# Shared-expert products, the last batches' routing and the row norms rescheduled in a fused attention and mixture-of-experts kernel

## The chip, the core and the metric

The kernel runs on one core of one Trainium2 chip. The metric is the time of one execution on the device in microseconds (us). All engines of the core are named as in the profile: PE (TensorE, matrix products) with PEld (its weight loads), DVE (VectorE), ACT (ScalarE), POOL (GpSimd) and SP (SyncE, which here only issues transfers). Each engine works through its own instructions in order and waits on semaphores that other engines raise.

## The reference

Four stages change a residual `x` of 4 batches x 256 tokens x 256 features, each after a layer norm. The change touches the end of the third and the whole fourth stage:

```python
x = x + _L0_xattn_ref(_layernorm(x), ctx_2048, mask)          # one wide attention over 1601 rows
x = x + _L0_ffn_ref(_layernorm(x), ...)                        # 16 experts, dense, plus shared
x = x + _L1_xattn_ref(_layernorm(x), ctx_2048, mask, ...)      # 16 heads of 16, 1601 keys
x = x + _L1_ffn_ref(_layernorm(x), ...)                        # 16 experts, top 2, plus shared
...
# inside _L1_xattn_ref, at its end
delta = rs * (ctx @ Wo.T + bo)
delta = (delta - mu) / jnp.sqrt(var + EPS_LN) * ln_gamma + ln_beta
...
# inside _L1_ffn_ref
logits = flat @ router_w.T
scores = jax.nn.softmax(logits, axis=-1)
_, topk_idx = jax.lax.top_k(logits + router_bias, TOPK)        # TOPK = 2
...                                                            # weights: chosen scores, normalized
for e in range(N_EXPERTS):                                     # 16 experts of width 128
    h = jax.nn.silu(flat @ Wu[e]) * (flat @ Wg[e])
    out = out + combine[:, e:e + 1] * (h @ Wd[e])
out = out + jax.nn.silu(flat @ Su[0]) * (flat @ Sg[0]) @ Sd[0] # shared expert of width 256
```

## The kernel before

**The attention loop.** The third stage is one loop over 208 units: 16 jobs (4 batches x 4 groups of heads) of 13 tiles of keys. For each unit x PE makes scores (`qk(x)`, L881), ACT takes their exponential (L1279), DVE clips it (`clip(x)`, L1659), and PE multiplies with the values (`pv`, L915) four units later. After a job DVE copies the product out (`evac`, L1665), PE transposes it (`flip`, L923), and DVE divides (`norm`, L1672 to L1677), which raises `cx_rdy`. What follows for a batch b (its tokens are row tiles t = 2b and t + 1) is hidden in the units of batch b + 1 by functions called `between`, one on each engine, with an order written out by hand in unit numbers `o` of 52 per batch: context transposed (`ctx_T`, L930) and multiplied by Wo (`ctx_out`, L937), `delta` with its statistics, `delta_gamma` (L1695), `delta_add` into the residual (L1701), `rows_stat` (L1705), `rows_mean` (L1710) at o = 39, `rows` (L1718, the normalized rows `xe`) at o = 43 and 45, `rows_T` on PE (L944) at o = 49, `rows_hi` on ACT (L1259) at o = 49 and `rows_lo` on DVE (L1723) at o = 50, which split the transposed rows in a rounded part `xTh` and a rest `xTl`. Between `rows_mean` and `rows`, POOL finds the inverse root with 13 small instructions (`inverse_root`, L351 to L359). In the next batch's units follow the router logits, the choice of two experts (fifteen small DVE instructions, `logits_ev` to `take_both`), `ranks` (L960, L963: each token's place within its expert), `slots_of` and `slots_to` (row addresses), and `rows_out` on POOL: four indirect transfers (L621) that scatter the two row tiles, 128 rows each, to each token's two places in the memory tensor `x_slots`.

**After the loop.** Batch 3 has no later units to hide in, and batch 2's choice is also made there. In order of the DVE: norm of the last job, `delta` and statistics, `delta_gamma`, `delta_add`, the row norms (here ACT takes the root), `rows`, `rows_lo`, then the choice for the four row tiles of batches 2 and 3 in one go, their slots, the counts (`all_counts`, L1046) turned into a list of 31 blocks of 128 slots (`nblk_` to `rb_i`, L1890 to L1913), in between and after it the shared expert's hidden products in four chunks (`shared_chunk`, L1899 and L1901), the softmax weights (`m_sum` to `m_w2`), and four additions of the shared expert's result to the residual (L1934). PE meanwhile makes the transposes and logits, 16 products with zeros that start the eight accumulators (L1015), and `shared_hidden(n)` (gate and up products, 6 matrix products each, of 512 tokens) and `shared_down(n)` (12 products). Each float32 product of this stage is made of three (`mm3`, L646, L647, L648) from rounded parts and rests. The shared expert's weights come with the expert weights when the loop has ended (SP waits for `cx_rdy`), and POOL splits them (`sh_hi` L633, `sh_lo` L635).

**The expert blocks.** For each of 31 blocks: SP loads 128 rows from `x_slots` (L544; it waits first for all scatters and for the block list), PE transposes them (L1064), gate and up product (L1078), ACT silu, DVE product (L1938), PE transpose and down product (L1092), DVE copy (L1949), POOL scatters them to `y_tokens` (L641). Then SP loads all rows back (`yg`), and DVE adds them to the residual with the softmax weights (L1963, L1965).

## Time and profile before

| | |
|---|---|
| median of 3 runs | 817.32 us (817.09 to 819.99) |
| the profiled execution, its own time | 816.02 us |
| its span, first to last instruction | 814.2 us |
| busy: PE, DVE, ACT, POOL | 707.8, 543.3, 396.5, 160.1 us |
| mean granted TensorE clock | 0.950 of full speed |
| attention loop, first exponential to the last job's context | 463.8 to 690.7 us |
| from there to the first expert block's gate and up product | 690.7 to 742.3 us |
| 31 expert blocks, to the last scatter issued | 742.3 to 798.0 us |

Times within the profile count from the span's first instruction. The shares are averages over four different stages, so that the table only says that PE works most of the time; what a microsecond is worth is read stage by stage.

### The profile page before, as it was taken

The numbers are of one execution on the slowest core, as the hardware profiler recorded it, in microseconds if no ns is written. First come the engines' busy times: TensorE is split into PE (matmuls) and PEld (weight loads), VectorE is DVE, ScalarE is ACT, GpSimd is POOL, SyncE is SP. The second block draws the span as 40 slices with busy tenths as digits, with TensorE's granted clock in tenths as the row PEclk, the third lists the DMA queues.
The fourth block names the chain that finished last, engine by engine and source line by source line (L and its number), as shares of the span: only waits on it lengthen the run. The fifth ranks groups of instructions, "written<-read, shape, count | busy, mean of one in ns | idle before, by whom it ended". The sixth has DMA issues, their size and how long they took to land.

```text
span 814.2 us, 14794 instructions
## 1 busy us (share of the span) xinstructions
PE 707.8 (87%) x5481; PEld 537.1 (66%) x5481; DVE 543.3 (67%) x1124; ACT 396.5 (49%) x558; POOL 160.1 (20%) x196
## 2 busy tenths in 40 slices
PE   4799999897859999999995599998998997587990
PEld 3689888796648888888885344454554554475880
DVE  6765565656676666666676377778888886655663
ACT  2624333233312322223322499999999996114540
POOL 5452625030100000000000000004024024231561
PEclk9999999998989999999998789999999998698995
DMA  7465464735306776767779369898687700812545
GB/s 231 129 208 214 162 220 130 270 104 178 96 23 221 238 248 206 262 211 245 240 172 198 60 112 191 133 127 166 96 137 144 108 2 30 345 53 74 162 144 180
DMA packets 57532, 131.67 MB, mean 162 GB/s; under 512 B 12433, under 2 KB 32785, under 8 KB 53889
## 3 DMA queue, kind: packets, MB, share of 16 engines
q1 hardware_dynamic: 54208, 123.46, 57.1%
q0 software_dynamic: 2256, 6.18, 2.1%
q10 hardware_dynamic: 1008, 1.25, 0.5%
q8 instruction: 37, 0.61, 0.4%
q14 instruction: 23, 0.18, 0.1%
HBM read 78.92 MB, written 48.79 MB: 157 GB/s over the span
## 4 chain that ended last, share of the span: by engine, by line
PE 53%; DVE 15%; issue 10%; ACT 9%; POOL 7%; DMA 4%; SPq 1%; POOLq 0%; DVEq 0%; ACTq 0%
PE ps L646 13%; PE ps L647 13%; PE ps L648 13%; ACT p L1279 5%; PE ps L915 5%; PE ps L881 3%; POOL y_tokens L641 3%; DVE p L1659 2%; DMA raw<-in_ctxT 1%; PE ps L1078 1%; DMA raw<-in_ctxN 1%; ACT cNh L1156 1%; PE ps L937 1%; PE ps L723 1%; POOL na L354 1%
## 5 line engine op out<-in xcount | busy, mean ns | idle before, releaser
L1279 ACT ACTIVATE p<-ps,kbias 128x1024 f32<-128x1024 f32 (+1 forms) x208 | 210.5, 1184 | 6.2 <-PE ps L881 6.2
L1659 DVE TENSOR_SCALAR p<-p 128x1024 f32<-128x1024 f32 (+1 forms) x208 | 142.6, 692 | 40.0 <-ACT p L1279 38.4
L915 PE MATMUL ps<-p,vsl 128*17 128x256 f32 (+1 forms) x1664 | 116.7, 392 | 3.6 <-DVE p L1659 3.6
L881 PEld LDWEIGHTS ps<-qst,kst 48*128 48x128 f32 (+1 forms) x832 | 60.4, 187 | 67.3 <-issue 34.6
L881 PE MATMUL ps<-qst,kst 48*128 48x256 f32 (+1 forms) x832 | 93.4, 324 | 11.5 <-DMA qst<-ql 5.9
L1219 ACT ACTIVATE hh<-h 128x512 fp32r<-128x512 f32 x50 | 31.6, 632 | 137.7 <-DVE h L1591 113.9
L351 POOL TENSOR_SCALAR nv<-mv 128x2 f32<-128x2 f32 x6 | 3.4, 561 | 423.7 <-DVE mv L1691 407.7
L646 PE MATMUL ps<-xTh,w_hi 128*128 128x512 f32 x200 | 80.0, 400 | 5.2 <-DVE h L1587 4.5
L648 PE MATMUL ps<-xTh,w_lo 128*128 128x512 f32 x200 | 79.3, 397 | 0.0
L647 PE MATMUL ps<-xTl,w_hi 128*128 128x512 f32 x200 | 79.2, 396 | 0.0
L915 PEld LDWEIGHTS ps<-p,vsl 128*17 128x17 f32 (+1 forms) x1664 | 37.2, 98 | 43.0 <-issue 9.1
L1593 DVE TENSOR_TENSOR hl<-h,hh 128x512 fp32r<-128x512 f32 x50 | 34.6, 692 | 36.6 <-ACT hh L1219 36.6
L646 PE MATMUL ps<-w_hi,hh 128*128 128x256 f32 x200 | 57.5, 288 | 1.5 <-DVE hl L1593 1.5
L1587 DVE TENSOR_TENSOR h<-silu,ps 128x512 f32<-128x512 f32 x50 | 34.4, 688 | 35.4 <-PE ps L648 23.2
L647 PE MATMUL ps<-w_lo,hh 128*128 128x256 f32 x200 | 57.2, 286 | 0.0
L648 PE MATMUL ps<-w_hi,hl 128*128 128x256 f32 x200 | 57.0, 285 | 0.0
L646 PEld LDWEIGHTS ps<-xTh,w_hi 128*128 128x128 f32 x200 | 37.9, 190 | 13.5 <-DVE h L1587 5.8
L589 POOL TENSOR_TENSOR cNl<-raw,cNh 128x1024 fp32r<-128x1024 f32 (+1 forms) x16 | 31.3, 1980 | 77.8 <-ACT cNh L1156 77.8
L648 PEld LDWEIGHTS ps<-xTh,w_lo 128*128 128x128 f32 x200 | 37.8, 189 | 9.0
L647 PEld LDWEIGHTS ps<-xTl,w_hi 128*128 128x128 f32 x200 | 37.9, 189 | 6.6
L646 PEld LDWEIGHTS ps<-w_hi,hh 128*128 128x128 f32 x200 | 38.7, 193 | 4.2 <-DVE hl L1593 1.9
L1215 ACT ACTIVATE silu<-ps 128x512 f32<-128x512 f32 x50 | 29.9, 598 | 21.6 <-PE ps L648 20.9
(290 smaller groups left out, 1530.0 us busy)
## 6 DMA issues: line engine op xcount, KB each, us to landing
x_slots<-blank SPq DMA_DIRECT2D x20, 1032.0 KB, 6.0
kst<-k_hi SPq DMA_DIRECT2D x64, 200.2 KB, 7.8
w_raw<-in_w SPq DMA_DIRECT2D x25, 384.0 KB, 3.6
v_one<-vst SPq DMA_DIRECT2D x4, 1768.0 KB, 9.0
vsl<-v_one SPq DMA_DIRECT2D x4, 1768.0 KB, 16.5
kst<-k_lo SPq DMA_DIRECT2D x32, 200.2 KB, 8.2
raw<-in_ctxN SPq DMA_DIRECT2D x12, 512.0 KB, 5.6
k_hi<-kh SPq DMA_DIRECT2D x24, 256.0 KB, 2.6
```

Of the source, the lines that this page charges most:

```text
L589: pool.tensor_tensor(cNl[:, c0:c0 + w, :], src, cNh[:, c0:c0 + w, :].bitcast(F32), ALU.subtract).then_inc(ctx_split, 1)
L646: e.matmul(o, lh, rh, start=first, stop=False, skip_group_check=True)
L647: e.matmul(o, lh, rl, start=False, stop=False, skip_group_check=True)
L648: return e.matmul(o, ll, rh, start=False, stop=last, skip_group_check=True)
L881: mm = pe.matmul(ps[0:rows, 2 * (x % RING) + t, c * SEQ:(c + 1) * SEQ], kst[r, job % KSL, c, m * P:m * P + rows], qst[r, b, 2 * g + c, :], ...
L915: mm = pe.matmul(ps[32 * j:32 * j + VW, 6 + job % 2, 0:SEQ], vsl[0:rows, b % 2, at_:at_ + VW], p32[0:rows, x % PBUF, (2 * t + c) * SEQ:(2 ...
L1215: act.activation(silu[:, half, :], ps[:, 4, :], ACT.Silu).then_inc(silu_rdy, 1)
L1219: act.activation(hh[:, half, :], h32[:, half, :], ACT.Copy).then_inc(hh_rdy, 1)
L1279: act.activation(p32[0:rows, x % PBUF, :], psf[0:rows, bank * 512:bank * 512 + 1024], ACT.Exp, scale=0.25, bias=kbias[0:rows, col:col + 1] ...
L1587: dve.tensor_tensor(h32[:, half, :], silu[:, half, :], ps[:, 5, :], ALU.mult).then_inc(mul1_rdy, 1)
L1593: dve.tensor_tensor(hl[:, half, :], h32[:, half, :], hh[:, half, :].bitcast(F32), ALU.subtract).then_inc(hl_rdy, 1)
L1659: dve.tensor_scalar(t, t, CLO, CHI, ALU.max, ALU.min).then_inc(p_clip, 1)
```

## The change

1. **Row norms.** `rows_mean` at o = 38 (was 39), `rows` at 45 and 46 (were 43 and 45), `rows_T` at 51 (was 49), `rows_hi` at 50 (was 49), `rows_lo` at 51 (was 50).
2. **Shared weights early.** SP loads them at the loop's first unit into `xn`, which is free then. DVE splits them with eight instructions in units 2 to 9 of job 2. SP's load after the loop and POOL's four instructions are gone.
3. **Batch 2 on its own.** Its logits go first in PE's order after the loop, DVE makes its choice ahead of `delta`, and its ranks, slots and scatter have steps of their own. The choice, slots and scatter of batch 3 follow later for two row tiles.
4. **Shared products by 512 tokens.** The first 512 tokens (batches 0 and 1) are ready in full before the loop ends. PE makes three of their four products (`gates(0,0)`, `ups(0,0)`, `gates(0,1)`) ahead of the last `rows_T`. The down products of a half are made in one go of 24 (`shared_down`), they start their own accumulators, and the 16 products with zeros are gone.
5. **Softmax weights last.** The exponential and DVE's eleven instructions on the softmax come after the expert blocks. The additions to the residual are spread: an expert block waits only for the addition that frees its accumulator.
6. Buffers move in SBUF, and the hidden tiles have four chunks (were two).

```diff
@@ sync
             for g in range(NG - 1):
                 queries(0, g)
+            sp.wait_ge(sc_rdy, 1)
+            for k in range(NSH1):
+                sp.dma_start(sh_raw[:, k * WC:(k + 1) * WC], a["w1"][k]).then_inc(d_in[0], 16)
...
             sp.wait_ge(cx_rdy, NJ)
-            for k in range(NSH1):
-                sp.dma_start(e_w[:, k, :], a["w1"][k]).then_inc(d_in[0], 16)
@@ gpsimd
-            for k in range(NSH1):
-                pool.wait_ge(d_in[0], 16 * NSH1)
-                pool.tensor_copy(sh_hi[:, k, :], e_w[:, k, :]).then_inc(d_w, 1)
-                pool.wait_ge(d_w, 2 * k + 1)
-                pool.tensor_tensor(sh_lo[:, k, :], e_w[:, k, :], sh_hi[:, k, :].bitcast(F32), ALU.subtract).then_inc(d_w, 1)
+            rows_out(NB - 1, NT - 4, NT - 2)
             pool.wait_ge(ln_xn, 4 * NT)
-            rows_out(NB - 1, NT - 4, NT)
+            rows_out(NB, NT - 2, NT)
@@ tensor, after the loop
             t = NT - 2
+            logits(NB - 2, ps[:, 5, :])
             pe.wait_ge(cx_rdy, NJ)
             for j in range(2):
                 ctx_T(t + j, 1, ps[:, j, :])
-            logits(NB - 2, ps[:, 7, :])
             for j in range(2):
                 ctx_out(t + j, j, 1, ps[:, 2 + j, 0:D])
+            ranks(NB - 1, NT - 4, NT - 2, ps[:, 1, :])
+            pe.wait_ge(d_w, 8)
+            gates(0, 0, 4)
+            ups(0, 0, 5)
+            gates(0, 1, 6)
+            pe.wait_ge(dl_ev, NT)
             for j in range(2):
-                rows_T(t + j, 1, ps[:, 4 + j, :])
-            logits(NB - 1, ps[:, 7, 2 * E:])
-            for n in range(4 * 4):
-                pe.matmul(psf[:, n * P:(n + 1) * P], zero[:], zero[:], start=True, stop=False, skip_group_check=True)
...
+                rows_T(t + j, 1, ps[:, 2 + j, :])
+            ups(0, 1, 0)
+            logits(NB - 1, ps[:, 7, :])
+            pe.wait_ge(silu_rdy, SC0 + 1)
+            gates(1, 0, 4)
+            pe.wait_ge(mul1_rdy, SC0 + 1)
+            ups(1, 0, 5)
+            pe.wait_ge(silu_rdy, SC0 + 2)
+            gates(1, 1, 6)
+            pe.wait_ge(pre_ev, NB - 1)
+            ranks(NB, NT - 2, NT, ps[:, 1, :])
+            pe.wait_ge(lg_ev, NB)
+            all_counts(ps[:, 7, 2 * E:3 * E])
+            pe.wait_ge(mul1_rdy, SC0 + 2)
+            ups(1, 1, 0)
+            pe.wait_ge(hl_rdy, SC0 + 2)
+            shared_down(0, 2)
+            pe.wait_ge(hl_rdy, SC0 + 4)
+            shared_down(1, 6)
@@ vector, in the loop and after it
-                    elif o == 39:
+                    elif o == 38:
                         rows_mean(b)
-                    elif o == 43:
+                    elif o == 45:
                         rows(t)
-                    elif o == 45:
+                    elif o == 46:
                         rows(t + 1)
-                    elif o == 50:
+                    elif o == 51:
                         rows_lo(t, 2, spare)
...
+                if job == 2 and 2 <= m < 10:
+                    (shared_hi if m < 6 else shared_lo)(m)
...
+            choose(t - 2, t, ps[:, 5, :])
             for j in range(2):
                 delta(t + j, 1, ps[:, 2 + j, :])
...
             rows(t + 1)
+            dve.wait_ge(pre_rdy, NB - 1)
+            slots_of(t - 2, t, ps[:, 1, :])
             for j in range(2):
-                rows_lo(t + j, 1, ps[:, 4 + j, :])
+                rows_lo(t + j, 1, ps[:, 2 + j, :])
+            slots_to(t - 2, t)
...
+            shared_mul(0, 5)
+            choose(t, NT, ps[:, 7, :])
+            shared_mul(1, 0)
             dve.wait_ge(pre_rdy, NB)
+            slots_of(t, NT, ps[:, 1, :])
+            slots_to(t, NT)
+            shared_low(0)
+            shared_low(1)
+            dve.wait_ge(pre_rdy, NB + 1)
...
+            for q in range(4):
+                x = resid[:, 2 * q:2 * q + 2, :].rearrange("p t d -> p (t d)")
+                dve.wait_ge(down_done, SC0 + q // 2 + 1)
+                dve.tensor_tensor(x, x, ps[:, (2, 3, 6, 7)[q], :], ALU.add).then_inc(add_rdy, 1)
```

## Rows read from the trace of the kernel before

**Rows 1.** Windows: from:to, length, busy us (count) per engine, clock, DMA share, GB/s.
```profile
695.00:700.00 5.00, 0.00 (x0) 0.00 (x0) 4.89 (x9) 0.30 (x1) 4.72 (x4) 0.80 1.00 396
...
705.00:710.00 5.00, 4.74 (x23) 4.77 (x23) 1.75 (x9) 0.00 (x0) 0.00 (x0) 0.50 1.00 391
...
750.00:797.00 47.00, 44.77 (x244) 36.97 (x242) 27.54 (x109) 22.10 (x81) 28.09 (x30) 1.00 0.50 147
```

**Rows 2.** Chain that ended last, pieces after the loop: start, us, what.
```profile
712.43 0.43 PE ps L648
...
733.86 1.28 ACT L1304
...
738.51 2.49 DVE resid L1934 x4
...
753.05 0.87 PE ps L1078 x4
...
754.67 0.86 PE ps L1078 x4
...
801.04 4.95 DMA yg<-y_tokens
```

**Rows 3.** Timeline, end of the loop: start, us, instruction, [idle before <-releaser].
```profile
656.82 24.14 ACT L1279 ACTIVATE p<-ps,kbias 128x1024 f32<-128x1024 f32 x24 [0.61 <-PE ps L881]
...
678.68 0.41 DVE L1718 TENSOR_SCALAR xe<-resid,mv,rstd 128x256 f32<-128x256 f32 x1 [2.02 <-POOL rstd L359]
...
682.75 0.60 ACT L1259 ACTIVATE xTh<-ps 128x512 fp32r<-128x512 f32 x1 [1.79 <-PE ps L944]
...
684.41 2.11 ACT L1279 ACTIVATE p<-ps,kbias 128x1024 f32<-128x1024 f32 x2 [1.06 <-PE ps L881]
...
689.05 0.42 DVE L1665 COPY oS<-ps 128x256 f32<-128x256 f32 x1 [1.60 <-PE ps L915]
```

**Rows 4.** Timeline, row norms of batch 0 (569 us) and batch 1.
```profile
569.40 0.60 ACT L1259 ACTIVATE xTh<-ps 128x512 fp32r<-128x512 f32 x1 [0.53 <-PE ps L944]
...
625.72 0.60 ACT L1259 ACTIVATE xTh<-ps 128x512 fp32r<-128x512 f32 x1 [1.16 <-PE ps L944]
```

**Rows 5.** Timeline, DVE and POOL at the last norms.
```profile
693.75 0.48 DVE L1681 SCALAR_TENSOR_TENSOR xn<-ps,rs,bo 128x256 f32<-128x256 f32 x1 [3.02 <-PE ps L937]
...
695.82 2.42 DVE L1695 SCALAR_TENSOR_TENSOR xn<-xn,mv,gam 128x256 f32<-128x256 f32 x2
...
696.02 1.94 POOL L635 TENSOR_TENSOR sh_lo<-e_w,sh_hi 128x768 fp32r<-128x768 f32 x1
...
698.35 2.79 DVE L1701 SCALAR_TENSOR_TENSOR resid<-xn,rstd,resid 128x256 f32<-128x256 f32 x2
...
702.65 0.74 DVE L1718 TENSOR_SCALAR xe<-resid,mv,rstd 128x256 f32<-128x256 f32 x2
...
704.26 0.85 DVE L1723 TENSOR_TENSOR xTl<-ps,xTh 128x256 fp32r<-128x256 f32 x2 [0.88 <-ACT xTh L1259]
```

**Rows 6.** Timeline, from the choice to the first expert block.
```profile
708.00 0.22 DVE L1744 COPY m_l<-ps 128x64 f32<-128x64 f32 x1 [2.89 <-PE ps L648]
...
711.54 0.23 DVE L1768 TENSOR_TENSOR sel<-one 128x64 fp32r<-128x64 f32 x1
...
718.24 0.17 DVE L1780 CAST pos_i<-pos_f 128x8 int32<-128x8 f32 x1
...
728.22 1.01 POOL L621 DMA_INDIRECT x_slots<-xe,pos_i  x1 [0.30 <-issue]
...
731.76 14.84 SPq L544 DMA_DIRECT2D xb<-x_slots  x7
...
742.32 2.07 PE L1078 MATMUL ps<-e_w,xbT 128*128 x4 [0.15 <-ACT xbT L1308]
```

**Rows 7.** Group of DVE instructions by form, over the span: count, busy us, mean ns.
```profile
L1901 DVE TENSOR_TENSOR hl_d<-h_d,hh_d 128x512 fp32r<-128x512 f32 x4 | 2.8, 692 | 2.8 <-ACT hh_d L1302 1.4 <-issue 1.4
```

**Rows 8.** The same view, from 600 to 690 us, in the loop.
```profile
L1695 DVE SCALAR_TENSOR_TENSOR xn<-xn,mv,gam 128x256 f32<-128x256 f32 x4 | 1.9, 479 | 0.0
```

More of the change, by code:

```diff
@@ L198, in build @@
             big_d = Dt("big_d", [P, NBLK, E])
[L199 to L201 removed]
+            m_p, m_e = Dt("m_p", [P, NT, E]), Dt("m_e", [P, NT, E])
+            eb_f = Dt("eb_f", [P, NBLK])
+            eb_i = Dt("eb_i", [P, NBLK], I32)
+            eb_r = Dt("eb_r", [P, NBLK])
+            y_c = Dt("y_c", [P, NBLK])
+            y_i = Dt("y_i", [P, NBLK], I32)
+            ob, rb_f = Dt("ob", [P, NBLK]), Dt("rb_f", [P, NBLK])
+            rb_i = Dt("rb_i", [P, NBLK], I32)
+            Dt("gap3", [P, 4050])
             gw_raw_d = Dt("gw_raw_d", [P, KT, E])
@@ L1002, in _, with gates, ups, shared_down @@
             flip(NJ - 1)
+            def gates(h, k, bank):
+                s = slice(h * 512, h * 512 + 512)
+                for q in range(KT):
+                    w = slice(q * 2 * P, q * 2 * P + P)
+                    mm = mm3(pe, ps[:, bank, :], sh_hi[:, k, w], sh_gl[:, k, w], xTh[:, q, s], xTl[:, q, s], q == 0, q == 1)
+                mm.then_inc(G_rdy, 1)
+            def ups(h, k, bank):
+                s = slice(h * 512, h * 512 + 512)
+                for q in range(KT):
+                    w = slice(q * 2 * P + P, (q + 1) * 2 * P)
+                    mm = mm3(pe, ps[:, bank, :], sh_hi[:, k, w], sh_gl[:, k, w], xTh[:, q, s], xTl[:, q, s], q == 0, q == 1)
+                mm.then_inc(U_rdy, 1)
+            def shared_down(h, bank):
+                for j in range(4):
+                    o = ps[:, bank + j // 2, (j % 2) * D:(j % 2 + 1) * D]
+                    s = slice(j * P, (j + 1) * P)
+                    for k in range(NSH1):
+                        mm = mm3(pe, o, hh_d[:, 2 * h + k, s], hl_d[:, 2 * h + k, s],
+                                 sh_hi[:, k, 2 * D:3 * D], sh_dl[:, k, :], k == 0, k == NSH1 - 1)
+                mm.then_inc(down_done, 1)
+            def all_counts(o):
+                for t in range(NT):
+                    mm = pe.matmul(o, ones[:], sel[:, t, :], start=t == 0, stop=t == NT - 1, skip_group_check=True)
+                mm.then_inc(pre_rdy, 1)
             t = NT - 2
+            logits(NB - 2, ps[:, 5, :])
             pe.wait_ge(cx_rdy, NJ)
@@ L1033, in shared_down @@
-            def shared_down(n):
-                k, half = n // 2, n % 2
-                pe.wait_ge(hl_rdy, SC0 + n + 1)
-                for j in range(4):
-                    t, s = 4 * half + j, slice(j * P, (j + 1) * P)
-                    mm = mm3(pe, ps[:, t // 2, (t % 2) * D:(t % 2 + 1) * D], hh_d[:, half, s], hl_d[:, half, s],
-                             sh_hi[:, k, 2 * D:3 * D], sh_lo[:, k, 2 * D:3 * D], False, False)
-                mm.then_inc(down_done, 1)
-            def all_counts():
-                cnt = ps[:, 7, 4 * E:5 * E]
-                for t in range(NT):
-                    mm = pe.matmul(cnt, ones[:], sel[:, t, :], start=t == 0, stop=t == NT - 1, skip_group_check=True)
-                mm.then_inc(pre_rdy, 1)
@@ L1049, in _ @@
-            shared_hidden(0)
-            ranks(NB - 1, NT - 4, NT, ps[:, 6, :])
-            all_counts()
-            for n in range(1, 2 * NSH1):
-                shared_hidden(n)
-                shared_down(n - 1)
-            shared_down(2 * NSH1 - 1)
+            ranks(NB - 1, NT - 4, NT - 2, ps[:, 1, :])
[4 more added lines that the diff above has]
+            pe.wait_ge(dl_ev, NT)
+            for j in range(2):
+                rows_T(t + j, 1, ps[:, 2 + j, :])
@@ L1293, in _, with shared_silu, shared_high @@
             for j in range(2):
-                rows_hi(t + j, 1, ps[:, 4 + j, :])
-            for n in range(2 * NSH1):
-                ct, half = SC0 + n, n % 2
-                act.wait_ge(G_rdy, ct + 1)
-                act.activation(silu_d[:, half, :], ps[:, 4, :], ACT.Silu).then_inc(silu_rdy, 1)
-                act.wait_ge(mul1_rdy, ct + 1)
-                if n >= 2:
-                    act.wait_ge(down_done, ct - 1)
-                act.activation(hh_d[:, half, :], h32_d[:, half, :], ACT.Copy).then_inc(hh_rdy, 1)
-            act.wait_ge(pos_rdy, NB)
-            act.activation(m_p[:].rearrange("p t e -> p (t e)"), m_e[:].rearrange("p t e -> p (t e)"), ACT.Exp).then_inc(s_exp, 1)
+                rows_hi(t + j, 1, ps[:, 2 + j, :])
+            def shared_silu(n, bank):
+                act.wait_ge(G_rdy, SC0 + n + 1)
+                act.activation(silu_d[:, n, :], ps[:, bank, :], ACT.Silu).then_inc(silu_rdy, 1)
+            def shared_high(n):
+                act.wait_ge(mul1_rdy, SC0 + n + 1)
+                act.activation(hh_d[:, n, :], h32_d[:, n, :], ACT.Copy).then_inc(hh_rdy, 1)
+            shared_silu(0, 4)
+            shared_silu(1, 6)
+            shared_high(0)
+            shared_silu(2, 4)
+            shared_high(1)
+            shared_silu(3, 6)
+            shared_high(2)
+            shared_high(3)
             def slots_ev(j):
```

139 lines of the change are left out of this document (67 added, 72 removed).

## The prediction

> **What bounds the kernel now.** First I read the timeline at the end of the attention loop. There ACT sets the pace: 24 exponentials follow each other without a gap, 1.006 us apart [rows 3]. Then ACT stands for 1.79 us until PE has transposed batch 2's normalized rows, and for 1.06 us more until PE has the next scores [rows 3]. PE is late because DVE is late: DVE stood 2.02 us for POOL's root ahead of `rows` [rows 3]. The same wait stands at the other two batches, with 0.53 and 1.16 us [rows 4]. So the loop is bound by ACT and has holes cut by the row norms.
>
> Second, the timeline and the windows after the loop. `cx_rdy` comes at about 690.7 (the last job's copy starts at 689.05 and flip and division take 1.7 us). The last norms run until DVE's `rows` end at 703.39 [rows 5]; for 695 to 700 us PE does nothing at all [rows 1], and this is the hole. PE then works at 1.2 GHz (clock 0.50 [rows 1]): a product of 128x512 takes 0.43 us [rows 2], half of it at 2.4 GHz. From 703.39 to the first expert product at 742.32 [rows 6] lies a chain of choice, slots, eight scatters, block list, shared products, softmax weights and additions. PE, the scatters and DVE all take part in it, and DVE's order decides: its four additions end at 741.0 [rows 2], and the expert blocks wait for the last.
>
> Third, the chain of waits in the expert blocks: one gate and up product starts 1.62 us after the other and nearly all pieces between are PE's [rows 2]. The change does not touch a block's work, so what is won before it is kept to the end, unless the clock changes.
>
> **Part by part.** Times on the right of an arrow are of the changed kernel, on the trace's time scale without what batches 0 and 1 give.
>
> *Row norms.* `rows_mean` comes a unit (1.0 us) earlier, so POOL's root is there a unit earlier, and DVE asks for it two units later. DVE's 2.02 us of waiting shrink to nothing. The second `rows` moves by one unit, PE's transposes by two, so that their rows lie ready about 2 us ahead. PE makes the last two scores ahead of the transposes, so that ACT needs no wait for either. Batches 0 and 1 give 0.53 + 1.16 = 1.7 us. What is queued behind the later `rows_T` are products with the values, which have four units of lead. For batch 2: exponential 205 ends at 680.96 [rows 3], then one exponential, `rows_hi` 0.60, the last exponential 1.0, clip 0.7, `rows_lo` 0.7: the last job's copy starts at 685.1 instead of 689.05, if PE stays at 2.4 GHz because its holes are gone. That gives 4.0 us; `cx_rdy` -> 686.8.
>
> *Shared weights in job 2.* Eight DVE instructions of 512 or 256 columns. The dearest kind near it, 128x512 from two inputs, takes 0.692 us [rows 7], so at most 5.5 us; I take 3.5, for half of them are casts and half are of 256 columns. DVE has 0.3 us free per unit (0.69 of 1.006), 2.4 us in eight units, less a norm, a copy and an addition. It falls behind by some 1.5 us, and the four units of lead cover this. Cost 0, at worst 3.5; I take 0.4. SP's two transfers of 0.4 MB each stand ahead of `keys(3)`, which waits for unit 13 anyway.
>
> *POOL's split is gone from the norms.* Two `delta_gamma` took 2.42 us and two `delta_add` 2.79 while POOL subtracted [rows 5]. In the loop one takes 0.479 [rows 8]. With pitches of 0.45 the four take 1.8 instead of 5.2: 3.4 us. The Trainium skill ("SBUF — State Buffer", Who interferes with whom) says that a DVE instruction with two SBUF inputs and a GpSimd instruction that reads SBUF exclude each other; the long rows agree. The same section says that descriptors of GpSimd's own DMAs can starve under DVE's copies; by that the scatters moved beside DVE's work would be longer, and I come back to it as a rival.
>
> *Batch 2's choice ahead of `delta`.* Its logits run after `flip`, in the 0.7 us until `cx_rdy` and a little beyond: 12 small products, 1.3 us -> done 687.4. Fifteen DVE instructions for four row tiles took 3.77 us (708.00 to 711.77 [rows 6]); for two tiles, with a pitch of 0.22, 3.3 -> 690.8. `delta` could have started at 689.2 (it waited for PE until 693.75 [rows 5]), so the choice delays it by 1.6. From there to the end of `rows` it was 9.64 us [rows 5], less 3.4 = 6.25 -> 697.05. From `cx_rdy` to `rows` it was 12.7 and becomes 10.3: 2.4 us.
>
> *Shared products in the hole.* After `ctx_out` (690.1) PE does six small rank products and 18 products of 128x512 at 0.23 us: 691.0 -> 696, before `rows_T` at 697. They fit, cost nothing on the path, and keep PE busy, so the later work should run at 2.4 GHz.
>
> *From `rows` to the first expert product.* `rows_lo` ends 1.7 us after `rows` as before [rows 5] -> 698.8. PE: `ups(0,1)` 1.3, logits 1.3 (2.9 before, at half the clock [rows 6]) -> 700.2 with the first product beginning while `rows_lo` still waits for `rows_hi`. Choice of two tiles 3.3 -> 703.5. PE has made three more chunks by 704.4, ranks 1.0 -> 705.4. Slots 0.8 and 0.6 -> `pos_i` 706.8 (718.41 before [rows 6]). Now DVE has 9.5 us without a pause: 17 instructions, of them four shared and three list ones of 0.67 to 0.71 us, by pitch: two rests 1.3, list to `off` 1.55, `end_` 0.25, product 0.7, `big_d` 0.7, product 0.7, `eb_f` 0.7, rest 0.7, the six small and two long ones to `rb_i` 2.25, last rest 0.7 -> 716.3. `shared_down(1)` waits for this last rest. Its 24 products of 128x256 are 2.8 us at 2.4 GHz and 5.1 at 1.2; PE has stood for about 5 us before it, as ahead of 742.32, where the clock was down: I take 4.4 -> 720.7. Transposes and copy 0.95 -> first expert product 721.65. From `rows` on that is 24.6 us instead of 38.9: 14.3 us. The softmax weights are part of it, 4.65 us between the table load and the additions [rows 2].
>
> *The scatters beside it.* Four instead of eight stand at the end. The pitch was 1.27; from `pos_i` 706.8 the last is issued by 712.5, and from the last issue's end (729.23) to SP's first load (731.76) it was 2.5 [rows 6] -> 715.1. Then SP needs `rb_i` (715.6) and a load, 3 us -> 718.7, under the 720.7 of PE, with 2 us to spare.
>
> *The blocks' start.* The first block's product took 2.07 us, later ones 0.87 [rows 2, 6]. With PE coming straight from `shared_down` the first blocks run at 2.4 GHz: 0.9 us.
>
> *Softmax weights last.* One exponential with its table load and eleven instructions, 4.65 us [rows 2], start on the old scale when ACT has done the last block, 31 blocks of 1.62 after 742.3 and an overlap of 1 to 2, near 794.6, so they end at 799.3. The loads of `yg` land at 806.0 [rows 2], the first near 803, so they cover it by 4 us. Without the cover it would cost those 4.65.
>
> *Sum.* 1.7 + 4.0 + 2.4 + 14.3 + 0.9 - 0.4 = 22.9 us, from 816.02 us of the profiled execution, 793.1. The median of before is 1.3 us above its profiled run, so 817.32 - 22.9 = 794.4; I say **794.5**. The terms with bounds: the loop's 5.7 may be 2 to 7; the split -3.5 to 0; `shared_down` +0.7 or -1.6; the hole's 3.4 from 2 to 4.
>
> **The rivals.**
>
> *The clock stays down through the hole.* For it: the clock did fall in this stretch, with a mean of 0.80 from 695 to 700 us and 0.50 from 705 on [rows 1]. Against it: it fell when PE had done nothing for some us, and this time is filled now. At 1.2 GHz the 18 products last 7.7 us instead of 4.2, `rows_T`, `ups` and logits 3 us more: the choice of batch 3 starts 5.3 us later: 799.8.
>
> *The loop gives nothing.* The wait moves with the norms: PE transposes in the last pair of units of a batch, ACT has two exponentials instead of three of lead, and waits again. For it: less lead. Against it: DVE's wait was the cause. 5.7 us stay in: 800.2.
>
> *The scatters become the bound.* POOL takes 1.01 us to issue one [rows 6]. Were each to be held up beside DVE so that it took 1.94, as POOL's subtraction did [rows 5], the first four (from 700.7) would end at 709.4 instead of 705.8, and the last four at 718.3. With 2.5 and 3 us for landing and load, PE would have its rows at 723.8 instead of 720.7: 797.6. For it: batch 2's four now lie beside DVE's densest work. Against it: the eight of before lay beside subtractions and products too, at 1.01.
>
> *Slower.* One mechanism: the expert blocks run at 1.2 GHz. They are PE's alone, 1.62 us each at clock 1.00 [rows 1, 2], so a block at half the clock would cost 1.6 us more. From 14 slow blocks of 31 on, the 22.9 us are eaten; all 31 give 844. For it: the new blocks follow on a wait of PE. Against it: before, the blocks began slow after such a wait too, and all from 750 us on ran at clock 1.00 [rows 1].
>
> *Nothing changes*: only if a wait of about 20 us took the place of the chain, and the profile shows none.
>
> **How the numbers follow.** Forecast 0.62, clock in the hole 0.15, loop gives nothing 0.12, scatters 0.07, slower 0.03, nothing 0.01. The likeliest has 790 to 798 from its bounds; the range takes in the two rivals near 800 and a few us for DVE's order: **790 to 803**. About 0.5% is what can be told from no change. Faster 0.96, same 0.01, slower 0.03.
>
> **What would show it.** Right: ACT without a wait before its last two exponentials; `delta_gamma` and `delta_add` at 0.48 us; clock 1.00 from `flip` to about 12 us after `rows`; the first expert product some 31 us after the last `cx_rdy` (51.6 before); DVE waiting for nothing of PE between `pos_i` and the last rest. Wrong: PE at 0.50 in the hole, ACT waiting for `rows_T` again, SP's first load later than `rb_i`, or DVE standing for logits longer than 3 us.

## The result and the profile after

| | before | after |
|---|---|---|
| median on the same chip, 4 runs each | 817.21 us (815.5 to 819.99) | 792.52 us (791.19 to 799.51) |
| ratio, 95% interval | | 0.971 (0.965 to 0.978) |
| the profiled execution, its own time and its span | 816.02, 814.2 us | 793.57, 791.8 us |

The prediction was 794.5 us, 790 to 803. To see where the time went, I cut each span at five events that any of these kernels has. The loop begins here with PE's first product on the queries' weights, ahead of the first exponential, and ends at the start of the last `cx`.

| stretch of the trace, us | before | after | change | predicted |
|---|---|---|---|---|
| span's start to the loop | 449.81 | 451.39 | +1.58 | 0 |
| loop | 240.63 | 234.77 | -5.86 | -5.7 + 0.4 |
| last `cx` to the first expert product | 51.88 | 35.14 | -16.74 | -16.7 (2.4 + 14.3) |
| first expert product to the first scatter into `y_tokens` | 6.86 | 5.31 | -1.55 | -0.9 |
| first to last of the 31 scatters | 47.87 | 48.22 | +0.35 | 0 |
| last scatter's issue to the end | 17.15 | 16.97 | -0.18 | 0 |

**End of the loop.** The timeline of ACT and of DVE in the kernel after, from 656 to 687 us; a row is start, duration, engine, line, and in brackets the idle time ahead of it with what ended it. They answer to [rows 3].

```profile
656.68 25.14 ACT L1294 ACTIVATE p<-ps,kbias 128x1024 f32<-128x1024 f32 x25 [0.62 <-PE ps L883]
681.62 0.68 ACT L1274 ACTIVATE xTh<-ps 128x512 fp32r<-128x512 f32 x1
682.11 1.19 ACT L1294 ACTIVATE p<-ps,kbias 65x1024 f32<-65x1024 f32 x1
...
679.24 0.41 DVE L1742 TENSOR_SCALAR xe<-resid,mv,rstd 128x256 f32<-128x256 f32 x1 [0.92 <-POOL rstd L364]
...
686.16 0.29 DVE L1701 TENSOR_TENSOR cx<-ps,r 128x128 f32<-128x128 f32 x1
```

ACT's waits of 1.79 and 1.06 us are gone: 25 exponentials, the copy `rows_hi` and the last exponential follow each other. DVE still stands for POOL's root, 0.92 us instead of 2.02. Its second `rows` end at 680.58 (680.17 + 0.41), PE transposes from 680.87 to 681.53, and ACT's copy starts at 681.62. Nobody is late, but the margins are 0.3 and 0.1 us and not the 2 us that the prediction gave the rows.

**The last norms.** The timeline of DVE, 692 to 697 us, which answers to [rows 5].

```profile
692.23 0.88 DVE L1719 SCALAR_TENSOR_TENSOR xn<-xn,mv,gam 128x256 f32<-128x256 f32 x2
...
693.22 0.88 DVE L1725 SCALAR_TENSOR_TENSOR resid<-xn,rstd,resid 128x256 f32<-128x256 f32 x2
...
695.62 0.74 DVE L1742 TENSOR_SCALAR xe<-resid,mv,rstd 128x256 f32<-128x256 f32 x2
```

The pairs that took 2.42 and 2.79 us beside POOL's subtraction take 0.88 each. This is 3.45 us, and `rows` end at 696.36.

**PE and its clock.** The windows of the kernel after, which answer to [rows 1] (busy time of each engine, then PE's granted clock, the share of the DMA engines' time, GB/s).

```profile
695.00:700.00 5.00, 4.27 (x26) 3.24 (x25) 3.42 (x14) 3.93 (x8) 0.69 (x1) 1.00 1.03 402
...
710.00:712.00 2.00, 0.51 (x5) 0.31 (x3) 1.93 (x4) 1.01 (x2) 1.69 (x2) 1.00 0.34 122
712.00:714.00 2.00, 0.00 (x0) 0.00 (x0) 1.90 (x6) 0.00 (x0) 0.43 (x1) 0.81 0.22 76
714.00:720.00 6.00, 4.76 (x22) 4.77 (x23) 2.79 (x8) 0.00 (x0) 0.00 (x0) 0.50 0.24 66
...
724.00:770.00 46.00, 46.00 (x253) 38.55 (x252) 28.37 (x113) 23.18 (x85) 25.96 (x27) 1.00 0.55 154
```

The hole is filled: clock 1.00 (2.4 GHz) where before it was 0.80 and then 0.50. It falls to 1.2 GHz once, in PE's wait for the last rest, and is up again when the blocks begin.

**From the addresses to the first block.** The chain of waits of the kernel after, 714 to 721 us.

```profile
714.41 0.18 DVE rb_i L1969
714.59 0.61 DVE hl_d L1939
...
715.24 0.58 PE ps L648
...
720.38 0.12 PE ps L650
720.75 0.39 ACT xbT L1330
721.15 0.15 issue
```

DVE's list and rests set the pace up to 715.2, then 24 down products that follow each other 0.213 us apart (the last three closer), and the first expert product starts at 721.30. SP's first load stood at 715.69, 1.1 us after the list was there:

```profile
711.46 0.97 POOL L627 DMA_INDIRECT x_slots<-xe,pos_i  x1 [0.31 <-issue]
...
715.69 3.74 SPq L550 DMA_DIRECT2D xb<-x_slots  x4
```

The last scatter's issue had ended 3.3 us before it. Where a scatter does set this load, it is 2.5 us, as before [rows 6], or 2.7, as in experiment 10, whose chain has 2.60 us from the issue of the last scatter until it has landed. By this the last one was there at about 714.06 (an estimate: 711.46 + 2.60), 0.5 us ahead of the end of `rb_i` (714.59). So the scatters are off the path, but by half a microsecond at this load.

### The profile page after: what moved, and what is told of

Same layout as the page of the kernel before. It is cut to its first block, busy times and chain, and to the rows that moved or that the text cites. A ratio compares the mean times of both kernels' runs of the same rounds, so it can differ in the third digit from the quotient of the medians.

```text
span 791.8 us, 14802 instructions
## 1 busy us (share of the span) xinstructions
PE 703.4 (89%) x5471; PEld 532.9 (67%) x5471; DVE 544.1 (69%) x1153; ACT 394.2 (50%) x557; POOL 164.9 (21%) x192
## 3 DMA queue, kind: packets, MB, share of 16 engines
HBM read 78.92 MB, written 48.79 MB: 161 GB/s over the span
## 4 chain that ended last, share of the span: by engine, by line
PE 56%; ACT 12%; DVE 11%; issue 10%; DMA 6%; POOL 4%; SPq 2%; POOLq 0%; ACTq 0%; DVEq 0%
PE ps L648 13%; PE ps L649 12%; PE ps L650 12%; ACT p L1294 8%; PE ps L917 5%; PE ps L1092 3%; PE ps L883 3%; DMA raw<-in_ctxN 2%; PE ps L1108 2%; DMA raw<-in_ctxT 2%; POOL cTl L608 1%; POOL cNl L595 1%; ACT cNh L1171 1%; PE ps L659 1%; DMA k_lo<-kl 1%
## 5 line engine op out<-in xcount | busy, mean ns | idle before, releaser
L1421 DVE SCALAR_TENSOR_TENSOR kl<-ps,bk,kh 128x512 fp32r<-128x512 f32 (+1 forms) x32 | 19.5, 631 | 30.8 <-ACT kh L1162 30.8
```

## The experiments

The executions of one set lie several us apart (791.19 to 799.51 us for the changed kernel), and two sets of one kernel differ too: the changed kernel gave 792.52 and, later, 794.51 us. The sets come from different chips: experiments 1 to 4 from one, 5, 6, the first 7 and 8 from another, and the second 7, 9 and 10 with the second set of the changed kernel from a third. So beside the medians I compare stretches of the traces, cut as above, and medians of different chips only by their ratio to the kernel before. "Loop" is the second stretch of the table, "middle" the third, "start" the fourth, "blocks" the fifth; medians are of 4 to 6 executions (10 in experiment 2), and each ratio is to the kernel before beside it.

| kernel | median, us | ratio to before (95%) | loop | middle | start | blocks |
|---|---|---|---|---|---|---|
| before | 817.21 | 1 | 240.63 | 51.88 | 6.86 | 47.87 |
| after | 792.52 | 0.965 to 0.978 | 234.77 | 35.14 | 5.31 | 48.22 |
| after, once more | 794.51 | 0.967 to 0.974 | 233.51 | 35.63 | 5.31 | 48.13 |
| 1 norms where they were | 802.56 | 0.975 to 0.985 | 242.41 | 34.96 | 5.29 | 52.12 |
| 2 norms alone, on before | 813.15 | 0.991 to 0.996 | 235.13 | 53.77 | 6.98 | 47.88 |
| 3 POOL beside the norms | 799.48 | 0.973 to 0.981 | 234.46 | 39.42 | 5.32 | 49.19 |
| 4 softmax weights first | 795.15 | 0.968 to 0.977 | 233.47 | 35.77 | 5.36 | 51.57 |
| 5 hole empty | 801.81 | 0.979 to 0.985 | 234.74 | 42.43 | 5.30 | 48.79 |
| 6 zeros in the hole | 798.79 | 0.976 to 0.982 | 234.49 | 38.90 | 5.30 | 50.63 |
| 7 zeros ahead of the down products | 797.04 | 0.975 to 0.979 | 233.48 | 33.56 | 5.28 | 50.61 |
| 7 once more | 794.82 | 0.965 to 0.973 | 237.51 | 33.16 | 5.26 | 48.97 |
| 8 last rest early | 794.11 | 0.969 to 0.974 | 234.80 | 33.74 | 6.81 | 50.36 |
| 9 last rest early, and zeros | 793.58 | 0.965 to 0.972 | 234.46 | 33.86 | 6.80 | 47.95 |
| 10 all eight scatters at the end | 797.51 | 0.971 to 0.978 | 233.49 | 37.53 | 6.80 | 47.94 |

**1. The norms where they were** (edit on the changed kernel, in the three `between` functions; experiment 2 is the reverse edit on the kernel before).

```diff
@@ tensor
-                    elif o == 51:
+                    elif o == 49:
                         pe.wait_ge(cx_rdy, y // MT)
                         rows_T(t, 2, spare)
@@ scalar
-                    elif o == 50:
+                    elif o == 49:
                         rows_hi(t, 2, spare)
@@ vector
-                    elif o == 38:
+                    elif o == 39:
                         rows_mean(b)
-                    elif o == 45:
+                    elif o == 43:
                         rows(t)
-                    elif o == 46:
+                    elif o == 45:
                         rows(t + 1)
-                    elif o == 51:
+                    elif o == 50:
                         rows_lo(t, 2, spare)
```

> The changed kernel with its row norms put back to the unit numbers of before (rows_mean 39, rows 43 and 45, transposes 49). Theory (DVE's wait for the root stops the loop): ACT waits again near 569, 625 and 682 us by 0.5, 1.2 and 1.8 us, PE falls to 1.2 GHz at the loop's end, and the kernel is 5.7 us slower than the changed one, so about 798.5 us and 18.8 us faster than before. Rival (the loop's gain came with another part, such as SP's order or the early weights): the time stays at 792.5 us.

> The kernel before with the new unit numbers of the row norms and nothing else. Theory: the same three waits go, the last job's context comes 5.7 us earlier, and the kernel takes 811.5 us (ratio 0.993). Rival (the later transposes only pay together with the rest): 817 us, ratio 1.000.

ACT's timeline at the loop's end, first experiment 1, then experiment 2:

```profile
684.74 0.60 ACT L1274 ACTIVATE xTh<-ps 128x512 fp32r<-128x512 f32 x1 [1.74 <-PE ps L946]
686.40 2.11 ACT L1294 ACTIVATE p<-ps,kbias 128x1024 f32<-128x1024 f32 x2 [1.06 <-PE ps L917]
```

```profile
656.96 25.16 ACT L1279 ACTIVATE p<-ps,kbias 128x1024 f32<-128x1024 f32 x25 [0.61 <-PE ps L881]
682.18 0.60 ACT L1259 ACTIVATE xTh<-ps 128x512 fp32r<-128x512 f32 x1
682.67 1.10 ACT L1279 ACTIVATE p<-ps,kbias 65x1024 f32<-65x1024 f32 x1
```

The waits come back with the old units and go with the new ones, on either kernel. The loop as a whole loses 7.6 us in experiment 1 and gains 5.5 in experiment 2, whose ratio of 0.993 is 5.4 us. But the loop's first units differ between traces whatever the norms: 13.9 or 15.2 us pass from its start to the first exponential, and the sixth to the eleventh exponential are 6.0 to 6.4 or 7.6 us apart (7.6 in the traces of the kernel after and of experiments 2 and 5, where PE's clock came up later). The stretch in which the norms lie, from the 93rd of the 208 exponentials to the last `cx`, is free of this. It takes 131.75 us before and 132.54 in experiment 1, 124.72 in both traces of the changed kernel, 124.69 to 124.96 in the other nine traces with its code, and 125.00 in experiment 2. So the new places are worth 7.0 us on this stretch, 6.8 of them on their own, and undoing them costs 7.8.

By the ratios (0.980 beside 0.971) experiment 1 as a whole is some 7 us slower than the changed kernel, more than the 5.7 expected. Its blocks also took 3.9 us longer (below), which the edit does not touch.

**3. POOL beside the norms.** POOL copies and subtracts the shared weights once more from the moment `delta` starts, into a tile of its own that nobody reads.

```diff
+            pool.wait_ge(d_w, 8)
+            pool.wait_ge(dl_ev, NT)
+            for k in range(NSH1):
+                pool.tensor_copy(spl[:], sh_hi[:, k, :].bitcast(F32)).then_inc(d_w, 1)
+                pool.wait_ge(d_w, 8 + 2 * k + 1)
+                pool.tensor_tensor(spl[:], sh_hi[:, k, :].bitcast(F32), sh_hi[:, 1 - k, :].bitcast(F32), ALU.subtract).then_inc(d_w, 1)
+                pool.wait_ge(d_w, 8 + 2 * k + 2)
             rows_out(NB - 1, NT - 4, NT - 2)
```

> The changed kernel, with two POOL casts and two POOL subtractions of 128x768 added at the last norms, started when DVE has made both deltas. Their result goes to an unused buffer. Theory (POOL and DVE's two-input instructions hold each other up): the two delta_gamma take some 2.4 us instead of 0.88 and the two delta_add 2.8 instead of 0.88, the path is 3.4 us longer, about 796 us. Rival (the long rows of before came from the weight transfers running at 400 GB/s, which run here too): the four stay at 0.48 us each and the time at 792.5 us.

DVE's timeline in it:

```profile
691.32 2.49 DVE L1728 SCALAR_TENSOR_TENSOR xn<-xn,mv,gam 128x256 f32<-128x256 f32 x2
...
693.92 2.84 DVE L1734 SCALAR_TENSOR_TENSOR resid<-xn,rstd,resid 128x256 f32<-128x256 f32 x2
```

The two pairs are back at 2.49 and 2.84 us, 3.6 more than 0.88 twice, and the middle is 4.3 us longer (3.8 beside the second trace of the changed kernel). Most of the rest is a wait of DVE of 0.64 us for PE's `ctx_out` ahead of the second `delta`, since PE's clock was 0.50 there. The weight transfers run beside the pairs in both kernels (402 GB/s from 695 to 700 us in the kernel after, where the pairs are fast), so they are not what made them long. The neighbour is the cause. The rule that the prediction took from the Trainium skill ("SBUF — State Buffer", Who interferes with whom) holds here in both directions: the same instructions, slow with POOL beside them, fast without.

**4. The softmax weights first.** The exponential and DVE's eleven instructions go back ahead of the four additions.

```diff
 @@ scalar, ahead of the expert blocks (was behind them)
+            act.wait_ge(pos_rdy, NB + 1)
+            act.activation(m_p[:]..., m_e[:]..., ACT.Exp).then_inc(s_exp, 1)
 @@ vector, ahead of the additions to resid (was behind the blocks)
+            dve.wait_ge(s_exp, 1)
+            link(dve.tensor_reduce(m_sum[:], m_p[:], AX.X, ALU.add))
...
+            link(dve.tensor_tensor(m_w2[:], m_w2[:], m_top[:], ALU.mult))
```

> The changed kernel with the softmax exponential and DVE's eleven softmax instructions put back ahead of DVE's four additions. Theory: they need 4.65 us, but shared_down(1) with its 5.3 us runs beside them, so that the additions of banks 6 and 7 end only 1 to 2 us later; with the silu table loaded again in the first block this makes 2 us, about 794.5 us. Rival (all 4.65 us were on the path, as the sum of the prediction took them): 797.2 us.

DVE's timeline in it, from the first to the last of the eleven and on to the additions:

```profile
712.44 0.29 DVE L1974 TENSOR_REDUCE m_sum<-m_p 128x8 f32<-128x128 f32 x1 [0.38 <-ACT m_p L1328]
...
715.26 0.17 DVE L1984 TENSOR_TENSOR m_w<-m_w,m_top 128x8 f32<-128x8 f32 x1
715.46 1.28 DVE L1988 TENSOR_TENSOR resid<-resid,ps 128x512 f32<-128x512 f32 x2
717.13 1.29 DVE L1988 TENSOR_TENSOR resid<-resid,ps 128x512 f32<-128x512 f32 x2 [0.38 <-PE ps L650]
```

DVE waits for PE's down products even behind the softmax: it fits under them. The middle is 0.1 to 0.6 us longer than in the two traces of the changed kernel. So the last place of the softmax is worth next to nothing beside down products of 5.3 us, and the theory's 2 us were too many.

**5 and 6. The hole.** In 5 the three shared products come behind `rows_T`, in 6 too, with 18 products with zeros in their old place.

```diff
             pe.wait_ge(d_w, 8)
-            gates(0, 0, 4)
-            ups(0, 0, 5)
-            gates(0, 1, 6)
+            for n in range(18):   # only in 6
+                pe.matmul(ps[:, 4, :], zero[:], xTh[:, 0, 0:512], start=True, stop=True, skip_group_check=True)
             pe.wait_ge(dl_ev, NT)
             for j in range(2):
                 rows_T(t + j, 1, ps[:, 2 + j, :])
+            gates(0, 0, 4)
+            ups(0, 0, 5)
+            gates(0, 1, 6)
             ups(0, 1, 0)
```

> The changed kernel with the three chunk products gates(0,0), ups(0,0) and gates(0,1) moved from ahead of the last rows_T to behind it, so that PE has nothing to do during the last norms. Theory: the 18 products (4.2 us at 2.4 GHz) now stand ahead of the logits of batch 3, and PE, idle for some 5 us, falls to 1.2 GHz, so that they, the logits and the next chunks take up to twice as long: 4.2 us plus 3 to 6 us, about 801 us. Rival (the hole's filling saves only the products' own time, the clock is not touched by an idle stretch of this length): 4.2 us, 796.7 us.

> The same as the kernel with the empty hole, but with 18 products of 128x512 with a zero matrix in the hole, into an accumulator that is written anew later. Theory: they do nothing but keep PE busy, the clock stays at 2.4 GHz, and what is left is the 4.2 us of the moved products: 796.7 us, and 3 to 6 us less than with the empty hole. Rival (the clock falls or stays for another reason than PE's idle time): the same time as with the empty hole.

Windows of PE, experiment 5, then 6:

```profile
695.00:700.00 5.00, 2.47 (x8) 0.61 1.03 403
700.00:705.00 5.00, 5.00 (x17) 0.71 0.99 385
```

```profile
695.00:700.00 5.00, 5.00 (x28) 1.00 1.03 401
700.00:705.00 5.00, 5.00 (x28) 1.00 0.66 255
```

The middle is 7.3 us longer with the hole empty and 3.8 longer with zeros in it. So the shared products in the hole are worth 3.8 us as work done there. Of the 3.5 us between the two experiments not all is the empty hole's. In experiment 5 the clock was already at 0.50 from 686 to 690 us, ahead of the hole, where the two kernels are the same; `rows` end 11.66 us behind the last `cx` instead of 10.18, so that 1.5 us were lost before the edit could act. This leaves 2.0 us for a clock that is kept at 2.4 GHz. The expected 3 to 6 us were too many.

**7, 8 and 9. The last wait.** PE stands for 4.7 us ahead of the last down products and makes them at 1.2 GHz. Experiment 7 fills the wait with 19 products with zeros, experiment 8 moves the last rest (`shared_low(3)`) ahead of the block list's end, experiment 9 does this and puts 10 products with zeros into what is left of the wait.

```diff
             shared_down(0, 2)
+            pe.wait_ge(silu_rdy, SC0 + 3)
+            for n in range(19):   # 10 in experiment 9
+                pe.matmul(ps[:, 4, :], zero[:], xTh[:, 0, 0:512], start=True, stop=True, skip_group_check=True)
             pe.wait_ge(hl_rdy, SC0 + 4)
             shared_down(1, 6)
 @@ vector, experiments 8 and 9
             shared_low(2)
+            shared_low(3)
             link(dve.tensor_scalar(eb_r[:], eb_f[:], -1.0, float(E), ALU.mult, ALU.add))
...
             dve.tensor_scalar(rb_i[:], rb_f[:], float(P), None, ALU.mult).then_inc(eb_rdy, 1)
-            shared_low(3)
```

> The changed kernel with 19 products of 128x512 with a zero matrix between the two shared_down, in the 4.6 us in which PE waits for the last rest and falls to 1.2 GHz. Theory: shared_down(1) takes 2.9 instead of 5.3 us, the first expert product starts 2.3 us earlier, about 790.2 us (ratio to the changed kernel 0.997). Rival (the rows of the first block from x_slots, or the additions, come no earlier): unchanged, since SP's first load lands at 717.7 us only if it is not later than in the trace.

> The changed kernel with 19 products with zeros ahead of the down products of the second half, once more, beside a control. In the trace they made the down products 2.9 instead of 5.3 us and the way from the last rest to the first expert product 2.0 us shorter. Theory (the fall of the clock costs 2 us on the path): 2 us below the control of this call. Rival (the gain is lost elsewhere, or is smaller than the scatter of executions): within 1 us of the control, or above it.

> The changed kernel with DVE's last rest (shared_low(3)) put ahead of the last seven instructions of the block list. shared_down(1) can start 2.1 us earlier, the block list and with it SP's first load end 0.7 us later. Theory (DVE's order sets the start of the expert blocks through shared_down): first expert product 2 us earlier or more, about 790.3 us. Rival (the block list and the load of the rows behind it are the bound): 0.7 us later, 793.2 us.

> The changed kernel with the last rest (shared_low(3)) ahead of the block list, and 10 products with zeros ahead of the second half's down products, so that these run at 2.4 GHz. Theory: PE would have its down products done near 715.5 and the row loads become the bound: block list 716.0, first load at PE near 719.5, first expert product 720.0 to 720.5 instead of 721.30, and the first blocks no longer at half the clock: 1 to 1.5 us below the control. Rival (PE's wait of about 4 us for the rows lowers the clock again, so that the first blocks run at 1.2 GHz and the gain is lost): within 0.5 us of the control.

PE's timeline in the second trace of experiment 7, then in experiment 8, then in 9:

```profile
712.76 4.61 PE L1068 MATMUL ps<-xTh,zero 128*128 128x512 f32 x19
717.64 0.39 PE L648 MATMUL ps<-sh_hi,hh_d 128*128 128x256 f32 x1 [0.27 <-DVE hl_d L1942]
721.40 0.44 PE L1079 MATMUL ps<-ident,xb 128*128 128x128 f32 x2 [0.44 <-DMA xb<-x_slots]
```

```profile
713.99 0.46 PE L648 MATMUL ps<-sh_hi,hh_d 128*128 128x256 f32 x1 [2.48 <-DVE hl_d L1939]
719.51 0.44 PE L1076 MATMUL ps<-ident,xb 128*128 128x128 f32 x2 [0.89 <-DMA xb<-x_slots]
```

```profile
711.64 2.50 PE L1068 MATMUL ps<-xTh,zero 128*128 128x512 f32 x10
719.75 0.44 PE L1079 MATMUL ps<-ident,xb 128*128 128x128 f32 x2 [2.36 <-DMA xb<-x_slots]
```

With zeros the middle is 1.6 to 2.5 us shorter, and the row loads are next: PE waits 0.44 us for them. The medians do not show it: 797.04 us once (a ratio of 0.977), and 794.82 beside 794.51 of the unaltered kernel on the same chip. In the first trace of 7 the blocks were 2.4 us longer than in the changed kernel, by the stalls described at the end. In the second the loop was 4.0 longer than in the kernel once more: 1.3 ahead of the first exponential and 2.7 in it, where PE stood for 1.50 and 1.63 us, in job 2, with nothing in the trace to wait for. Neither stretch is touched by the edit. So the gain is seen in its place and not in the total.

In 8 and 9 the down products end early, PE then waits for the rows (0.89 and 2.36 us), and the first blocks run at 1.2 GHz (clock 0.50 from 722 to 724 us in both): "start" is 6.8 instead of 5.3 us. Middle and start together are 40.55 and 40.66 us, against 40.45 and 40.94 in the changed kernel. What one gains the other gives back, and 9 stood at 793.58 beside 794.51 on the same chip, within what sets differ by. The theories of both fell in the total. The first expert product did come 1.3 to 1.9 us sooner behind the last `cx`, but PE's wait had moved to the rows, and the clock fell in it.

**10. All scatters at the end.** Batch 2's choice stays where it is, but POOL waits for batch 3's addresses too.

```diff
+            pool.wait_ge(pos_rdy, NB)
             rows_out(NB - 1, NT - 4, NT - 2)
```

> The changed kernel, but batch 2's four scatters wait until batch 3's addresses are there too, so that all eight stand at the end as in the kernel before. Theory (batch 2's choice on its own pays because four scatters fewer stand at the end): addresses 706.0, eight issues of about 1.1 us plus the waits, the last issued near 717.3, SP's first load near 719.8 instead of 715.7, first expert product near 723.5 instead of 721.3: 2 us above the control. Rival (all eight are hidden behind the block list and the down products): the same time as the control.

Last scatter on POOL, first load on SP, and PE's transposes of the rows:

```profile
712.64 0.97 POOL L627 DMA_INDIRECT x_slots<-xe,pos_i  x1 [0.30 <-issue]
```

```profile
716.27 7.63 SPq L550 DMA_DIRECT2D xb<-x_slots  x7
```

```profile
718.44 0.44 PE L1077 MATMUL ps<-ident,xb 128*128 128x128 f32 x2 [1.41 <-DMA xb<-x_slots]
```

SP's first load comes 5.55 us after `rb_i` instead of 1.28, PE waits 1.41 us for the rows, and the first blocks run at half the clock again. Middle and start are 3.4 us longer than in the second trace of the changed kernel, and the median is 3.0 us above its own on the same chip. The theory's 2 us left out the second effect. So the choice of batch 2 ahead of `delta` does pay, through its scatters: with eight at the end they bound the start of the blocks.

**What no experiment takes apart.** Middle and start together went from 58.74 to 40.45 us, by 18.3. Undone one at a time, the split beside the norms costs 4.3, the hole 7.3 (5.8 without the time lost ahead of it), the scatters 3.4 and the softmax at most 0.6. These need not add up, but if they do, some 3 to 4 us are left for the 16 products with zeros that are gone, the spread additions and the smaller steps. For these there is only the trace of the kernel after.

## Why the prediction was right, and where it was not

*Row norms and the loop's end.* Predicted 1.7 + 4.0 us. The loop of the profiled execution shows 5.9, but this close agreement is luck: it is 7.0 from the norms less 1.2 that this trace lost at the loop's start, where PE's clock was still 0.50 until 477 us; the second trace of the changed kernel had 1.00 from 475 us on, and its loop is 7.1 us shorter than before. Counted by exponentials, batches 0 and 1 gave 1.1 and 1.9 us instead of 0.53 and 1.16, and the last part 4.1. The term took one wait of ACT at each batch, but behind each stands a second of 0.34 us for PE's scores. The reason given, ACT waiting for PE for DVE for POOL's root, is shown by the waits that come and go. A detail was wrong: DVE's wait for the root did not shrink to nothing but to 0.92 us.

*Shared weights in job 2.* I took 0.4 us; nothing of it shows in this trace: ACT makes 51 exponentials without a gap from 479.88 us on, and the casts took 0.42 and 0.28 us. In three later traces with the same code (experiments 6, 8 and the second 7) PE stood in job 2 for 0.8 to 1.6 us once or twice, with nothing in the trace to wait for, and ACT fell 0.8 to 3.2 us behind. The first of these stands lies ahead of DVE's first cast, which speaks against the casts as the cause, but the two traces without the early weights (before and experiment 2) show no such stand; whether the weights have a part in it is open.

*POOL's split and batch 2's choice.* Predicted 3.4 for the split, found 3.45. The choice ahead of `delta` took 3.3 us (686.97 to 690.27), as predicted. From `cx_rdy` to the end of `rows` it is 9.9 us (686.45 to 696.36), where 10.3 was predicted.

*The hole.* The 18 products ran from 691.02 to 695.44 at 2.4 GHz (691 to 696 predicted). The rival "the clock stays down" is not as far off as this trace says. In the second trace of the changed kernel the clock was 0.50 from 687 to 689 us, and in experiment 3, whose hole is filled too, from 686 to 695. Both times it was 1.00 again, and the 18 products were done, before the last `rows_T` (690 and 695.54 us, and 695 and 698.83 in experiment 3). So the filled hole does not keep the clock from falling ahead of it, but in all these traces the clock is back when the work on the path begins. In the empty hole the clock cost 2.0 us, and 1.5 more ahead of it, where the rival said 5.3.

*From `rows` to the first expert product.* Predicted 24.6, found 24.94 us. Two errors inside cancel in part. `shared_down(1)` took 5.3 us, not 4.4: the clock did fall in the wait, and all but its last few products ran at 1.2 GHz; my value lay between the two levels, where the stretch is nearly all at the lower. DVE's list and rests took 9.0 us instead of 9.5.

*The softmax.* The prediction counted 4.65 us of it among the 14.3. That attribution fell: experiment 4 shows 0.1 to 0.6 us, since the down products of 512 tokens now stand on the path in its place and cover it. The sum was not hurt, because it was made forward, from the new chain. At the end the weights are covered as said, with 4.62 us to spare:

```profile
776.32 0.17 DVE L2012 TENSOR_TENSOR m_w<-m_w,m_top 128x8 f32<-128x8 f32 x1
781.11 0.48 DVE L2017 SCALAR_TENSOR_TENSOR resid<-yg,m_w,resid 128x256 f32<-128x256 f32 x1 [4.62 <-DMA yg<-y_tokens]
```

*The scatters.* Hidden, as forecast. One issue took 0.97 to 1.37 us at the end, not the rival's 1.94 (longer ones, up to 3.37 us, stand in the loop, where nobody waits). Yet the bound is near: SP's load has 0.5 us to spare over the last scatter, and in experiment 10 four more scatters cost 3 us. The sign of being wrong "SP's first load later than `rb_i`" came true by the letter, as the load starts 1.1 us behind the end of `rb_i`; but it follows `rb_i`, while in experiment 10, where the scatters hold it up, the distance is 5.4 us.

*The blocks' start.* Predicted 0.9, found 1.55: the first block's four products took 1.13 us instead of 2.07, and the next blocks ran faster as well.

*A number that did not follow.* The sentence on what would show it said some 31 us from the last `cx_rdy` to the first expert product; the sum itself has 10.3 + 24.6 = 34.9, and 34.85 was found. The 31 was a slip.

*Level.* The early stages, which the change does not touch, took 1.6 us longer in this profiled execution, and the span is 22.4 us shorter where 22.9 were summed; from the loop on it is 24.0. The medians differ by 24.7. As two sets of the changed kernel differ by 2.0, these figures are not evidence of a gain beyond the sum. That the terms sum so well is in part chance: the norms gave 1.3 us more than predicted and the blocks' start 0.6 more, while 1.2 went at the loop's start.

## What to carry to other kernels

Make the sum forward along the new chain, not by crediting each removed piece: what is taken off the path is worth only the distance to what stands next to it, as with the softmax here. Compare a stretch over several traces before its size is believed: the norms' stretch repeats within 0.3 us where the loop as a whole wanders by 4. Filling a hole of PE counts twice, for the work done in it and for the clock that the later work finds; and when a wait is shortened, look at the next one (here the row loads) before hoping for the total. A neighbour on POOL can make a DVE instruction with two inputs in SBUF about three times as long (2.49 and 2.84 beside 0.88 us for a pair), which is seen by comparing the same instruction at two places.

## What was not expected of the hardware

**A scatter of 3.37 us.** POOL's timeline in the kernel after, where batch 2's norms end in the loop, then in experiment 2, then in the kernel before:

```profile
679.74 3.37 POOL L627 DMA_INDIRECT x_slots<-xe,pos_i  x1 [0.54 <-issue]
```

```profile
680.30 3.36 POOL L621 DMA_INDIRECT x_slots<-xe,pos_i  x1 [0.54 <-issue]
```

```profile
679.19 1.42 POOL L621 DMA_INDIRECT x_slots<-xe,pos_i  x1 [0.54 <-issue]
```

DVE ran clips and row norms without a gap beside it. This is no chance of one trace. In each of the twelve traces with the norms at their new places the first of the four scatters behind batch 1's norms takes 3.22 or 3.23 us, and the first behind batch 2's 3.36 or 3.37. In the kernel before and in experiment 1, with the old places, they take 1.73 and 1.42. So moving the norms made them long; they cost nothing, as nobody waits for them. The Trainium skill ("SBUF — State Buffer", Who interferes with whom) says that DVE's copies can starve POOL's descriptors; these rows would fit, but which DVE instruction holds the scatter up, if one does, was not tested.

**The blocks stand at fixed places.** In the kernel before and in experiment 2, which has its blocks, no two scatters into `y_tokens` are more than 1.7 us apart. In all twelve traces with the new block code some are, and mostly at the same ones of the 31: behind the 1st, 10th, 13th, 16th to 18th, 20th, 23rd or 27th, with up to 3.5 us between two. From the first scatter to the last this makes 0.1 to 4.2 us. The chain of waits of experiment 4 at the 20th:

```profile
755.70 1.07 PE ps L1092 x4
756.76 0.02 issue
756.79 0.29 ACT sb_ L1336
757.07 0.02 issue
757.10 0.30 DVE hb L1992
757.39 0.04 issue
757.44 0.33 PE ps L1100
```

At other blocks the chain stays on PE, whose gate and up products are 0.87 us. Here ACT starts `sb_` 1.84 us after its previous instruction and then makes the next `sb_` 0.59 us later, so the first seems overdue (the last gate and up products before these had ended at 754.94); DVE and PE follow late, and no row shows what held ACT. The clock was 1.00. Since the places are the program's and the size changes from one execution to the next (48.13 and 48.22 us in the two traces of the changed kernel, 52.12 in experiment 1), it explains part of the scatter of the medians. PE's stands in the loop's job 2, told of above, are alike: 28.8 to 29.2 and 39.9 to 40.8 us behind the first exponential, in three traces. The cause of both stays open. The change loses 0.3 us in the blocks in its own two traces, and up to 4.2 in others.

**The clock fell after a shorter wait too.** In experiment 8 PE stood for 2.48 us ahead of 713.99, and from 714 to 716 us its clock was 0.54; in the changed kernel the wait was 4.72 us. I had expected the fall in the long wait alone. At the loop's end PE had two waits of 0.63 and 0.55 us in the second trace of the changed kernel, ahead of 683.38 and 684.56, and from 687 us its clock was 0.50 though it was busy; in the first trace they were 0.41 and 0.55 us and it stayed at 1.00.
